# The order of two sweeps over keys and values across heads, and where their sums are divided

## The chip, the cores and the metric

The kernel runs on one core of a Trainium2 chip. The metric is the device time of one launch in microseconds (us). A core has TensorE (PE, matrix products, with PEld for its weight loads), VectorE (DVE), ScalarE (ACT), GpSimd (POOL) and SyncE (SP), which here only starts DMA transfers. Each engine runs its own list of instructions in order; they wait for one another by semaphores.

## What is computed

Two transformer blocks on 896 tokens (16 x 56) of width 256 with a context of 24000 rows (16 x 1500). The change concerns the first block's cross attention and the projection behind it. All queries see all keys, in 16 heads of width 16, with values, keys, queries and attention weights rounded to 8 bits:

```python
q = _fq_sym(q, axis=-1)
k = _fq_sym(k, axis=-1)
v = _fq_sym(v, axis=2)
attn = jnp.einsum('bhqd,bhkd->bhqk', q, k)
attn = jax.nn.softmax(attn.astype(jnp.float32), axis=-1)
attn = _fq_unsigned(attn, axis=-1)
out = jnp.einsum('bhqk,bhkd->bhqd', attn, v)
out = jnp.transpose(out, (0, 2, 1, 3)).reshape(B, N, C)
return out @ Wp + bp
```

`_fq_unsigned` scales each row of weights by its own largest one, so every query's maximum over all 24000 keys is needed before its weights can be rounded. After this come a mixture of experts with 34 experts, a scan over the context (done here beside the last head), and a second mixture.

## The kernel before

Stages follow one another with a barrier between: queries, keys and values, `attention` (650 to 4994 us of the profile), `first_block` (normalisation, projection, experts), `second_block`. The change touches `attention` and the start of `first_block`.

**Two sweeps.** Each head is swept twice over its keys. The first sweep finds each query's maximum; the second makes the weights and multiplies them with the values. They run side by side: while head h1 is in its first sweep, head h2 = h1 - 1 is in its second. A sweep has 8 chunks (NCH) of 24 steps (CT), 192 steps for a head; a step is one tile of 125 keys.

**Second sweep, per step.** PE makes two score products (448 queries each, L719) into three rotating banks; ACT takes their exponential into `e` (L911); POOL rounds both halves into `r` (L1114); five to six steps later (LAG) PE adds 12 products into the sums `psav` (L746 and L753), which hold four partial sums: two sets of steps and two halves of the queries, 17 rows each, the last of them the softmax's denominator. The exponential's shift comes in as six extra rows of `q2`.

**First sweep.** Per chunk 42 pieces (UNITS): one product of 128 queries with 500 keys (L731) into one of four rotating banks `ps1`, and its maximum by DVE (L968). `pieces` spreads them over the steps: in ordinary chunks over all 24 (7 in 4 steps), in chunk 0 over steps 2 to 23, and in chunk 7 over steps 0 to 17. Then DVE reduces the head's maxima and splits the shifts into three bf16 parts (`shifts`, L980 to L989), PE turns them into rows at step 22 (`shift_rows`, L783), and DVE copies these into `q2` (L995). Twice a chunk PE and DVE also pass a correction of the values through a `ps1` bank (`sum_values`, L807, and `value_sums`, L1004, steps 15 and 19); these two marks serve below to cut the trace into chunks.

**Head change.** PE finishes the old head's sums in step 4, ACT copies them to `av` (`copy_sums`, L927, behind the exponentials of step 4), PE waits for that copy (L820), clears `psav` (L765) and goes on. After step 5, `turn_sums` multiplies `av` with a folding matrix `fold` (L773): that adds the two sets of steps and turns the result so that tokens lie on partitions. DVE divides by the denominators (`head_result`, L1032 and L1034), and ACT's queue stores the head's 16 columns in DRAM (`store_head`).

**Loop.** Heads 0 and 1 are written out; a hardware loop of 7 passes with two heads each follows, then the last head's second sweep alone, beside which DVE weighs the context for the second block. SP's list loads, per chunk, the first sweep's keys, the values, the second sweep's keys, and in chunk 0 both query tiles.

**First block.** It loads the stored rows `h` (896 KB), multiplies them by the values' scales on DVE (L1374), turns them with 16 products (L186), copies them (L192) and projects.

## Time and profile before

| | us |
|---|---|
| median of three runs | 5639.08 |
| lowest, highest | 5627.64, 5639.2 |
| profiled execution | 5629.81 |
| its span, first to last instruction | 5628.5 |
| stage `attention` in it | about 4344 |

The page gives each engine's busy share, the clock granted to TensorE in slices, and costly groups of instructions. The stage table gives the same for any window. A timeline lists instructions in order of time; an idle time stands in brackets, with what ended it (`PEq L709` is PE's own list at a wait in line 709). All times below are from the one profiled execution.

### The profile page before, as it was taken

Reading aid. Unit: us, or ns where it says so; the run is one execution under the profiler, and the core shown is the slowest. Engines: PE = TensorE matmul, PEld = TensorE weight load, DVE = VectorE, ACT = ScalarE, POOL = GpSimd, SP = SyncE. Lnnn points to the kernel's source line nnn. Section 1 sums busy time; section 2 is a strip of 40 time slices with the busy share of each in tenths; the row PEclk is TensorE's granted clock in tenths of the full one; section 3 lists DMA queues with packets and bytes.
Section 4 is the critical chain, followed back from the end, with each engine's and each line's share of the span. In section 5 each row is a group of like instructions: output and inputs, shape, how many; then the busy total and the mean of one; then the engine's idle time right before and its main releaser. Section 6 shows DMA issues by size and latency. Waiting matters only on the chain. (4 is left out here: it accounts for less than half of the span.)

```text
span 5628.5 us, 168594 instructions
## 1 busy us (share of the span) xinstructions
PE 5190.6 (92%) x53204; PEld 1990.4 (35%) x53204; DVE 4323.5 (77%) x7292; ACT 3881.7 (69%) x6380; POOL 3599.3 (64%) x3762
## 2 busy tenths in 40 slices
PE   4888599999999999999999999999999999969969
PEld 2444222333333333333333333333333332225535
DVE  6888698988989898898989888898988862234444
ACT  1444305988989898898989899898989985620000
POOL 1555604877878787787878788788878876620000
PEclk8999657999999999999999999999999985559979
DMA  2655311111111111111111111111111112211101
GB/s 83 182 180 182 106 44 28 32 27 33 30 30 32 28 32 27 33 27 32 30 29 32 27 29 30 28 32 33 27 33 28 31 44 78 78 40 30 31 16 29
DMA packets 242806, 267.97 MB, mean 48 GB/s; under 512 B 48397, under 2 KB 223645, under 8 KB 241946
## 3 DMA queue, kind: packets, MB, share of 16 engines
q1 hardware_dynamic: 176570, 202.39, 14.4%
q10 hardware_dynamic: 65376, 54.68, 3.1%
q8 instruction: 471, 7.72, 0.6%
q14 instruction: 389, 3.19, 0.2%
HBM read 173.41 MB, written 82.06 MB: 45 GB/s over the span
## 5 line engine op out<-in xcount | busy, mean ns | idle before, releaser
L911 ACT ACTIVATE e<-ps_sweep,sk 125x448 f32<-125x448 f32 x6144 | 3543.8, 631 | 525.3 <-ACTq L910 432.4
L968 DVE TENSOR_REDUCE unit_max<-ps_sweep 128x1 f32<-128x500 f32 x5376 | 3243.2, 669 | 409.1 <-DVEq L967 363.2
L1114 POOL TENSOR_SCALAR r<-e 125x896 f32<-125x896 f32 x3072 | 2882.2, 952 | 852.7 <-POOLq L1113 484.2
L719 PE MATMUL ps_sweep<-q,k 54*128 54x448 bf16 x6144 | 2067.9, 371 | 34.7 <-PEq L709 24.8
L731 PE MATMUL ps_sweep<-k,q 48*128 48x500 bf16 x5376 | 1771.9, 394 | 48.8 <-PEq L730 36.5
L753 PE MATMUL ps_av<-e,zt 126*17 126x224 f32 x24576 | 1810.5, 372 | 0.0
L746 PE MATMUL ps_av<-r,vt 125*16 125x224 f16 x12288 | 875.2, 275 | 14.7 <-PEq L739 4.8
L731 PEld LDWEIGHTS ps_sweep<-k,q 48*128 48x128 bf16 x5376 | 362.3, 94 | 1269.6 <-issue 1256.8
L719 PEld LDWEIGHTS ps_sweep<-q,k 54*128 54x128 bf16 x6144 | 551.6, 94 | 703.9 <-issue 611.0
L753 PEld LDWEIGHTS ps_av<-e,zt 126*17 126x17 f32 x24576 | 648.1, 98 | 6.0 <-issue 1.1
L746 PEld LDWEIGHTS ps_av<-r,vt 125*16 125x16 f16 x12288 | 302.1, 86 | 837.0 <-issue 837.0
L397 PE MATMUL ps_kv<-wkv,cx 128*125 128x512 f32 x768 | 353.0, 614 | 18.6 <-PEq L395 18.6
L1268 ACT ACTIVATE gate<-ps_gate 96x896 f32<-96x896 f32 (+1 forms) x50 | 45.6, 913 | 414.7 <-ACTq L1267 414.7
L1004 DVE COPY zt<-ps_sweep 32x192 f32<-32x192 f32 x256 | 93.1, 364 | 287.4 <-DVEq L1003 285.5
L1436 POOL MEMSET sel<- 16x896 f32 x1 | 0.8, 835 | 416.1 <-POOLq L71 416.1
L1122 POOL TENSOR_TENSOR vr<-vr,v_inv 125x192 f32<-125x192 f32 x256 | 151.7, 593 | 173.0 <-issue 164.1
L467 POOL TENSOR_TENSOR kq<-kparts,k_scale 125x1024 f32<-125x1024 bf16 x48 | 96.7, 2014 | 203.7 <-POOLq L466 203.7
L1276 DVE TENSOR_TENSOR hid<-ps_up,gate 96x896 f32<-96x896 f32 (+1 forms) x50 | 54.3, 1087 | 223.6 <-DVEq L1275 223.6
L491 ACT ACTIVATE kparts<-kq 125x1024 bf16<-125x1024 f32 x48 | 50.7, 1057 | 246.7 <-ACTq L490 246.7
L1130 POOL TENSOR_SCALAR vt<-vr 125x192 f16<-125x192 f32 x256 | 219.6, 858 | 0.5 <-POOLq L1128 0.3
L397 PEld LDWEIGHTS ps_kv<-wkv,cx 128*125 128x125 f32 x768 | 146.8, 197 | 189.9 <-issue 189.9
L406 PE MATMUL ps_krows<-ident_b,kparts 125*128 125x125 bf16 x1536 | 107.6, 236 | 106.6 <-PEq L403 106.6
(184 smaller groups left out, 2645.4 us busy)
## 6 DMA issues: line engine op xcount, KB each, us to landing
k_rows<-krows ACTq DMA_DIRECT2D x48, 1000.0 KB, 6.6
k<-k_rows SPq DMA_DIRECT2D x128, 281.2 KB, 4.0
k<-k_rows SPq DMA_DIRECT2D x384, 93.8 KB
cx<-in_ctxT SPq DMA_DIRECT2D x48, 500.0 KB, 4.4
v_raw<-kv SPq DMA_DIRECT2D x24, 1000.0 KB
vr<-v_raw SPq DMA_DIRECT2D x128, 187.5 KB
cb<-in_ctxT SPq DMA_DIRECT2D x16, 1500.0 KB, 6.4
gu_w<-in_gu SPq DMA_DIRECT2D x34, 192.0 KB, 2.3
```

The source lines that it names most:

```text
L397: last = pe.matmul(psk[:, i, :], cx[u][:, c, i * KT:(i + 1) * KT], wkv[:, c, :], start=(c == 0), stop=(c == NC - 1))
L406: last = pe.transpose(pst[:, b, i, 0:KT], parts[u][:, i, b * P:(b + 1) * P], ident_b[0:KT, 0:KT])
L467: pool.tensor_tensor(q4, ints(u), per_head(of_step(k_scale, n)), ALU.mult).then_inc(kq_ready, 1)
L719: pe.matmul(ps2[(2 * i + g) % 3][:, 0:HALF], k2[u][:, i * KT:i * KT + P], q2[y][:, g * HALF:(g + 1) * HALF], start=True, stop=True, tile_p ...
L731: pe.matmul(ps[:, 0:SB], q1[y][rows, b * QB:(b + 1) * QB], k1[u][rows, at * SB:(at + 1) * SB], start=True, stop=True, tile_position=(ROWS1 ...
L746: last = pe.matmul(psav[c:c + HDIM, lo:hi], vt[u][:, i + s, :], words[:, g, 2 * lo:2 * hi:2], start=False, stop=False, skip_group_check=Tr ...
L753: last = pe.matmul(psav[c:c + WIDE, lo:hi], zt[u][0:ONES_ROW + 1, i + s, :], e[(i + s) % SLOTS][0:ONES_ROW + 1, g, lo:hi], start=False, st ...
L911: act.activation(e[i % SLOTS][0:KT, g, :], ps2[(2 * i + g) % 3][0:KT, 0:HALF], ACT.Exp, scale=sk[u][:, i:i + 1]).then_inc(e_wrote, 1)
L968: top = dve.tensor_reduce(unit_max[:, b, bass.ds(j * NPIECE + at, 1)], ps[:, 0:SB], axis=AX.X, op=ALU.max)
L1114: pool.tensor_scalar(r[i % SLOTS][:, :, :], e[i % SLOTS][0:KT, :, :], 1.0, HALFWORD, ALU.mult, ALU.add)\
L1122: pool_done(pool.tensor_tensor(part, part, v_inv[:, bass.ds(h * HDIM, HDIM)].rearrange("p (o d) -> p o d", o=1) .to_broadcast([KT, VTILES, ...
L1130: pool_done(pool.tensor_scalar(vt[u][:, tiles, :], vr[:, tiles, :], ROUND, ROUND, ALU.add, ALU.subtract))
```

## The change

**Order of the first sweep.** The 336 pieces of a head are no longer dealt out by chunk. The last 12 steps of a head, 180 to 191, are taken out: in nine of them (EARLY) one piece of the *following* head is made, so that 327 pieces of a head remain for its steps 0 to 179 (MAIN). Right after the head's last piece, at step 180, DVE starts the shifts, now in three portions at steps 180, 181 and 183 with early pieces between, and PE turns them at the end of step 186. The values' corrections move to steps that have one piece. In the first head, 336 pieces are dealt over its steps 0 to 179.

**Sums.** `fold`, `turn_sums`, `head_result` and `store_head` go. ACT copies `psav` one step earlier in its list (before the exponentials of step 4), and SP stores the copy unturned: eight DMAs a head, issued in chunk 2, of four 16 x 448 sums and four rows of denominators. `first_block` loads them (1.8 MB), adds the two sets, inverts the denominators, spreads them over each head's 16 rows by a product with a selection matrix, multiplies, and has the values' scales in the projection's weights `wp` instead.

**Loop.** Six passes instead of seven; heads 14 and 15 are written out behind it, since head 15 has no follower (`more` false).

**SP's list.** Both query tiles of a head were loaded in chunk 0 behind the second sweep's keys; now the first sweep's come right behind its keys, and the second sweep's (which wait until the head before has left the tile) in chunk 1.

```diff
+    SCORES = NCH * UNITS
+    EARLY = (1, 0, 1, 0, 1, 1, 0, 1, 1, 1, 1, 1)
+    STEPS = NCH * CT
+    MAIN = STEPS - len(EARLY)
+    TURNED = len(EARLY) // 2
...
-        def pieces(i, at, end):
-
-            return 0 if i < at else min(UNITS, -(-UNITS * (i + 1 - at) // (end - at)))
-
-        def span_of(second, head_start, last):
-            return START if head_start and second else 0, CT - (LAG + 1 if last else 0)
+        def pieces(step, second, more):
+            ahead = sum(EARLY) if second else 0
+
+            def done(n):
+                return ahead - (-(SCORES - ahead) * n // MAIN)
+            if step < MAIN:
+                return [(False, n) for n in range(done(step), done(step + 1))]
+            lo = sum(EARLY[:step - MAIN])
+            return [(True, n) for n in range(lo, lo + EARLY[step - MAIN])] if more else []
+
+        def value_steps(j, second, more):
+            few = [i for i in range(SLOTS + 7, CT) if len(pieces(j * CT + i, second, more)) < 2]
+            return (few[0], few[-1]) if len(few) > 1 else (SLOTS + 7, CT - 2)
...
+            def store_sums(h):
+                sp.wait_ge(av_kept, 1).then_inc(av_kept, -1)
+                for c in range(4):
+                    sp.dma_start(attn_sums[c // 2, c % 2, bass.ds(h * HDIM, HDIM), :],
+                                 av[c * QUAD:c * QUAD + HDIM, :]).then_inc(av_stored, 16)
+                    sp.dma_start(attn_z[c, bass.ds(h, 1), :], av[c * QUAD + HDIM:c * QUAD + WIDE, :])\
+                      .then_inc(av_stored, 16)
...
             over_heads(sp, head)
+            store_sums(HEADS - 1)
+            sp.wait_ge(av_stored, 128).then_inc(av_stored, -128)
...
             def copy_sums():
                 act.wait_ge(sums_done, 1).then_inc(sums_done, -1)
+                act.wait_ge(av_stored, 128).then_inc(av_stored, -128)
                 act.activation(av[:, :], psav[:, 0:HALF], ACT.Copy).then_inc(av_ready, 1)
...
-                            if i == LAG - 1:
-                                copy_sums()
-                            if i == LAG + 3:
-                                store_head(finished)
+                        if head_start and finished is not None and i == LAG - 2:
+                            copy_sums()
...
+                        if first and step == MAIN:
+                            head_max(h1)
+                        if first and step == MAIN + 1:
+                            high_part()
+                        if first and step == MAIN + 3:
+                            other_parts()
...
+            pe.wait_ge(z_ready, 1).then_inc(z_ready, -1)
+            for c in range(NC):
+                for g in range(2):
+                    last = pe.matmul(ps[:, 2 * c + g, 0:HALF], head_sel[:, c * P:(c + 1) * P], z[0][:, g, :],
+                                     start=True, stop=True)
...
             dve.wait_ge(bp_landed, 16).then_inc(bp_landed, -16)
-            dve.wait_ge(attn_landed, 16).then_inc(attn_landed, -16)
-            dve.tensor_tensor(h[:, :, :], h[:, :, :], over_tokens(v_scale[0:TT, :], DIM), ALU.mult)\
-               .then_inc(a_ready, 1)
-            dve.wait_ge(a_turned, 1).then_inc(a_turned, -1)
-            copy_transposed(hT, ps).then_inc(aT_ready, 1)
+            dve.wait_ge(z_landed, 32).then_inc(z_landed, -32)
+            dve_done(dve.tensor_tensor(z[0][:, :, :], z[0][:, :, :], z[1][:, :, :], ALU.add))
+            dve.reciprocal(z[0][:, :, :], z[0][:, :, :]).then_inc(z_ready, 1)
+            dve.wait_ge(w_landed, 32).then_inc(w_landed, -32)
+            dve.wait_ge(scales_turned, 1).then_inc(scales_turned, -1)
+            for c in range(NC):
+                last = dve.tensor_tensor(wp[:, c, :], wp[:, c, :], psb[:, 0, c:c + 1].to_broadcast([P, DIM]), ALU.mult)
+            dve_done(last)
+            dve.wait_ge(attn_landed, 64).then_inc(attn_landed, -64)
+            dve_done(dve.tensor_tensor(attn[0][:, :, :, :], attn[0][:, :, :, :], attn[1][:, :, :, :], ALU.add))
+            dve.wait_ge(z_spread, 1).then_inc(z_spread, -1)
+            for c in range(NC):
+                last = dve.tensor_tensor(hT[:, c, :].rearrange("p (g n) -> p g n", g=2), attn[0][:, c, :, :],
+                                         ps[:, 2 * c:2 * c + 2, 0:HALF], ALU.mult)
+            last.then_inc(aT_ready, 1)
```

DVE's list at the end of a head's first sweep in the loop's first head. Before, with the maxima of this head (L968), the shifts (L980 to L989), a values' correction (L1004) and the copies into `q2` (L995):

```order
L968 TENSOR_REDUCE unit_max<-ps_sweep_3 128x1
L980 TENSOR_REDUCE run_max<-unit_max 128x7
L981 ISA
L981 TENSOR_TENSOR shift<-run_max,sq 128x7
L983 TENSOR_SCALAR shift<-shift 128x7
L984 CAST shift_parts<-shift 128x7
L985 TENSOR_TENSOR shift<-shift,shift_parts 128x7
L986 CAST shift_parts<-shift 128x7
L987 TENSOR_TENSOR shift_parts<-shift,shift_parts 128x7
```

Now, where the maxima (L973) between are already the following head's:

```order
L973 TENSOR_REDUCE unit_max<-ps_sweep_0 128x1
L985 TENSOR_REDUCE run_max<-unit_max 128x7
L986 ISA
L986 TENSOR_TENSOR shift<-run_max,sq 128x7
L988 TENSOR_SCALAR shift<-shift 128x7
L973 TENSOR_REDUCE unit_max<-ps_sweep_1 128x1
L991 CAST shift_parts<-shift 128x7
L992 TENSOR_TENSOR shift<-shift,shift_parts 128x7
L973 TENSOR_REDUCE unit_max<-ps_sweep_2 128x1
L995 CAST shift_parts<-shift 128x7
L996 TENSOR_TENSOR shift_parts<-shift,shift_parts 128x7
```

The shifts begin six steps earlier and are cut apart by two maxima; four maxima of the next head stand ahead of the copies into `q2`.

PE's list around the turning of the shifts at the end of the loop's second head. Before, with scores (L719), sums (L746, L753) and the shifts' products (L783):

```order
L746 MATMUL ps_av<-r,vt 16x224 x4
L753 MATMUL ps_av<-e,zt 17x224 x4
L719 MATMUL ps_sweep_0<-q_0,k_1 128x448
L783 MATMUL ps_sweep_1<-ident_b,shift_parts 6x128 x4
L783 MATMUL ps_sweep_2<-ident_b,shift_parts 6x128 x3
L719 MATMUL ps_sweep_1<-q_0,k_1 128x448
L746 MATMUL ps_av<-r,vt 16x224 x4
L753 MATMUL ps_av<-e,zt 17x224 x4
L719 MATMUL ps_sweep_2<-q_0,k_1 128x448
L624 REGISTER_ALU
L624 COMPARE_AND_BRANCH
```

Now, with scores (L747), sums (L777, L784), the shifts' products (L810) and pieces of the next head (L762):

```order
L762 MATMUL ps_sweep_3<-k_0,q_0 128x500
L747 MATMUL ps_sweep_2<-q_0,k_1 128x448
L747 MATMUL ps_sweep_0<-q_0,k_1 128x448
L777 MATMUL ps_av<-r,vt 16x224 x4
L784 MATMUL ps_av<-e,zt 17x224 x4
L747 MATMUL ps_sweep_1<-q_0,k_1 128x448
L810 MATMUL ps_sweep_0<-ident_b,shift_parts 6x128 x4
L810 MATMUL ps_sweep_1<-ident_b,shift_parts 6x128 x3
L747 MATMUL ps_sweep_2<-q_0,k_1 128x448
L777 MATMUL ps_av<-r,vt 16x224 x4
L784 MATMUL ps_av<-e,zt 17x224 x4
L762 MATMUL ps_sweep_2<-k_0,q_0 128x500
```

The products stand five steps ahead of the head's end instead of one, and pieces stand before and behind them.

PE's list in steps 5 and 6 of the loop's second head. Before, with the clearing (L765) and the folding (L773):

```order
L765 MATMUL ps_av<-zeros 32x448 x4
L746 MATMUL ps_av<-r,vt 16x224 x4
L753 MATMUL ps_av<-e,zt 17x224 x4
L731 MATMUL ps_sweep_2<-k_0,q_1 128x500
L719 MATMUL ps_sweep_2<-q_0,k_0 128x448
L773 MATMUL ps_sweep_3<-fold,av 112x64 x2
L773 MATMUL ps_sweep_0<-fold,av 112x64 x2
L731 MATMUL ps_sweep_1<-k_0,q_1 128x500
```

Now:

```order
L801 MATMUL ps_av<-zeros 32x448 x4
L777 MATMUL ps_av<-r,vt 16x224 x4
L784 MATMUL ps_av<-e,zt 17x224 x4
L762 MATMUL ps_sweep_0<-k_0,q_1 128x500
L747 MATMUL ps_sweep_2<-q_0,k_0 128x448
L762 MATMUL ps_sweep_1<-k_0,q_1 128x500
L747 MATMUL ps_sweep_0<-q_0,k_0 128x448
```

The folding is gone from between the pieces; the wait for the copy ahead of the clearing stays.

## Rows read from the trace of the kernel before

**Rows 1.** Page: clock granted to TensorE, 40 slices of the span, tenths.

```profile
PEclk8999657999999999999999999999999985559979
```

**Rows 2.** Stages: window, its us, busy us (instructions) per engine, clock, DMA share, GB/s.

```profile
2404.06:2577.43 173.37, 172.76 (x2281) 62.70 (x2280) 157.30 (x265) 164.76 (x288) 149.35 (x169) 1.00 0.14 31
...
2577.43:2610.08 32.65, 32.22 (x392) 11.08 (x389) 30.95 (x53) 28.84 (x50) 26.26 (x30) 1.00 0.14 31
...
3859.15:3894.00 34.85, 31.42 (x390) 11.93 (x390) 25.79 (x51) 27.95 (x50) 24.22 (x28) 1.00 0.15 30
...
2366.74:2404.06 37.32, 33.94 (x390) 12.78 (x390) 26.21 (x52) 27.88 (x50) 24.14 (x28) 0.91 0.13 28
...
2610.08:2654.94 44.86, 38.10 (x390) 12.86 (x390) 26.44 (x52) 28.08 (x50) 24.45 (x28) 0.77 0.12 25
```

**Rows 3.** Line L980 on DVE, one a head: ns min/median/max, first and last start.

```profile
L980 DVE TENSOR_REDUCE run_max<-unit_max x16: 502/502/504, 897.7 to 4594.2; 128x7 f32<-128x336 f32 x16
```

**Rows 4.** PE timeline, the undisturbed head change: start, us, line, tiles, [idle before].

```profile
3868.70 0.55 PE L783 MATMUL ps_sweep<-ident_b,shift_parts 128*6 128x128 bf16 x7 [1.00 <-PEq L781]
...
3871.22 0.35 PE L719 MATMUL ps_sweep<-q,k 54*128 54x448 bf16 x1 [0.80 <-ACT e L911]
...
3877.58 0.37 PE L731 MATMUL ps_sweep<-k,q 48*128 48x500 bf16 x1 [0.64 <-DVE unit_max L968]
...
3879.41 0.37 PE L765 MATMUL ps_av<-zeros 125*32 125x448 bf16 x4 [0.72 <-PEq L820]
...
3880.62 1.00 PE L773 MATMUL ps_sweep<-fold,av 128*112 128x64 f32 x8
```

**Rows 5.** DVE timelines: end of the first head (POOL idle), and of two later heads.

```profile
898.98 0.18 DVE L984 CAST shift_parts<-shift 128x7 bf16<-128x7 f32 x1
...
2371.16 0.50 DVE L980 TENSOR_REDUCE run_max<-unit_max 128x7 f32<-128x336 f32 x1 [0.42 <-DVEq L91]
...
2373.12 0.96 DVE L984 CAST shift_parts<-shift 128x7 bf16<-128x7 f32 x1
...
2375.81 0.17 DVE L989 COPY shift_parts<-shift_parts 128x7 bf16<-128x7 bf16 x1
...
2588.89 21.16 DVE L968 TENSOR_REDUCE unit_max<-ps_sweep 128x1 f32<-128x500 f32 x36 [0.44 <-PE ps_sweep L731]
```

**Rows 6.** Stages: four steps of a denser chunk 0, and of an ordinary one.

```profile
2404.06:2409.26 5.20, 5.20 (x67) 1.86 (x65) 5.14 (x10) 4.80 (x9) 4.66 (x6) 1.00 0.01 3
...
2433.03:2438.04 5.01, 4.91 (x66) 1.85 (x64) 4.57 (x9) 4.63 (x9) 4.47 (x6) 1.00 0.00 0
```

**Rows 7.** PE timeline, first score after the loop's branch.

```profile
2625.45 0.53 PE L719 MATMUL ps_sweep<-q,k 54*128 54x448 bf16 x1 [3.76 <-PEq L709]
```

**Rows 8.** Stages: one chunk of the last head, second sweep alone.

```profile
4733.30:4779.22 45.92, 45.92 (x339) 10.50 (x338) 10.13 (x12) 27.94 (x48) 29.49 (x29) 0.50 0.24 80
```

**Rows 9.** PE timeline, first turn of the key scales in the first head.

```profile
700.81 1.04 PE L797 MATMUL ps_sweep<-ident_b,t_parts 125*128 125x125 bf16 x8 [20.80 <-PEq L791]
```

**Rows 10.** SP timeline: three issues in a row.

```profile
2628.16 1.24 SPq L650 DMA_DIRECT2D k<-k_rows  x3
```

**Rows 11.** Timeline from the last sums to the next stage, all engines.

```profile
4985.03 0.55 ACT L927 ACTIVATE av<-ps_av 128x448 f32<-128x448 f32 x1 [5.99 <-ACTq L926]
...
4988.89 1.86 PE L892 MATMUL ps_sweep<-ctx_sum,w_in 128*128 128x16 f32 x8 [2.06 <-PEq L889]
...
5003.28 2.29 DVE L1374 TENSOR_TENSOR h<-h,v_scale 112x2048 f32<-112x2048 f32 x1 [9.43 <-DVEq L1373]
...
5009.09 2.09 DVE L192 COPY hT<-ps_a 128x896 f32<-128x896 f32 x2 [3.51 <-DVEq L1376]
```

**Rows 12.** DMA issues around there: tiles, queue, count, KB each, us to landing.

```profile
h<-attn_rows SPq DMA_DIRECT2D x1, 896.0 KB, 7.5
...
w_out<-in_W_outT SPq DMA_DIRECT2D x1, 256.0 KB, 3.9
```

**Rows 13.** A reciprocal of 256 columns on DVE.

```profile
L1016 DVE RECIPROCAL v_inv<-v_scale x1: 1753/1753/1753, 872.2 to 872.2; 125x256 f32<-125x256 f32 x1
```

198 lines of the change are left out of this document (89 added, 109 removed).

## The prediction

> **What bounds the kernel now.** Read the page's clock row first: TensorE has nearly full clock through the loop, and half in the first and the last head [rows 1]. Then the stage table, then the timelines at a head change. In an ordinary stretch everything is full: six chunks between the same mark (L1004) of chunk 0 and chunk 6 take 173.37 us, 28.90 us a chunk or 1.204 us a step, and PE is busy for 172.76 us of them at full clock (first row of [rows 2]). ACT stands close behind: 164.76 us for 288 exponentials, 0.572 us each, so 1.144 us for the two of a step; DVE has 157.30 us. Nothing in the change shortens such a step.
>
> Sixteen heads' reductions start 3696.5 us apart from first to last [rows 3], 246.4 us a head. Eight ordinary chunks would be 231.2 us. The other 15.2 us a head are the subject. They lie in two places [rows 2]. From chunk 6's mark to chunk 7's it takes 32.65 us, 3.75 too long: 42 maxima are asked for in 18 steps, and DVE runs 36 of them without a gap in 21.16 us, 0.588 us each [rows 5], more than PE needs. From chunk 7's mark to the next head's it takes 34.85, 37.32 or 44.86 us: 5.95, 8.4 or 16.0 too long, 11.5 us as a mean over the heads (15.2 - 3.75).
>
> The undisturbed change (34.85 us, clock 1.00) opens up in [rows 4]: PE waits 1.00 us for the shifts, turns them for 0.55, waits 0.80 for ACT, whose supply had run dry, 0.64 at the end of the sums, 0.72 for the copy, clears `psav` for 0.31 (3879.41 to the next sums) and folds for 1.00: 5.0 of the 5.95. In the 37.32 row the same idle times are followed by a granted clock of 0.91, 1.2 GHz for a part of the stretch; that is the other 2.5 us. In the 44.86 row PE also stands 3.76 us behind the loop's branch [rows 7] and the mean clock is 0.77. What a half clock costs: a chunk of the last head, all at 0.50, takes 45.92 us [rows 8], 1.913 us a step against 1.204, so 0.37 us lost in each us spent there.
>
> **The change, part by part.** The sum is made against the profiled 5629.8 us, 9.3 below the median of the runs.
>
> *Maxima of chunk 7.* The squeeze goes: -3.75 a head.
>
> *Shifts.* On DVE they take from 2371.16 to 2375.98 [rows 5], 4.8 us. Now they start at step 180 and PE asks for them at the end of step 186, seven steps or 8.1 us later at 1.15 each. Ahead of their end stand two early maxima (1.2 us): 0.7 us of lag, 4.8 and 1.2 are 6.7 us. So PE does not wait, ACT does not run dry, and only the 0.55 us of products stay: -1.8 a head, and -0.6 more for what follows them. What is late next is DVE's copy into `q2`, but five steps with early pieces stand between it and the head's start.
> The cast L984 takes 0.96 us there and 0.18 us where POOL has nothing to do [rows 5]. The Trainium skill (SBUF — State Buffer, "SBUF: two separate sides") says that VectorE and GpSimd share one port pair as an exclusive lock held for the whole instruction, which would explain that; by it the shifts would still wait for POOL's roundings in their new place, and the trace's 4.8 us already has such waits in it.
>
> *Early pieces and density.* Nine pieces in twelve steps leave PE free to follow ACT: 12 x (1.204 - 1.15) = -0.6. The price is that 327 pieces stand in 180 steps, where the old spacing would have 315: twelve more. Two stretches of four steps price one more maximum: with ten DVE instructions 5.20 us, with nine 5.01 [rows 6], so 0.19 us, and 12 x 0.19 = +2.3 a head. Bounds: a maximum costs nothing where ACT sets the pace (a little under 0.1 by the spread between steps with one and two pieces), and 0.588 us where DVE has no gap. DVE would be busy for 26.2 + 1.6 x 0.588 = 27.2 us of a 29 us chunk, so it is nearer to the first.
>
> *Sums.* Folding goes (-1.00), and the copy one place earlier in ACT's list ends before PE asks for it (-0.7). The end of the sums (0.64) and the clearing (0.31) stay, with a little around them: I keep 1.6 us a head. Less idle time also means, I expect, no half clock at a change without a branch: the stretch that stayed at 1.00 had the same waits as those that fell, and of these only one is left. SP's eight issues a head cost 8 x 0.42 us [rows 10] in chunk 2, where its next load has most of a chunk to spare: nothing. The moved query loads: `q1` is issued around step 157 and needed at 180; nothing.
>
> *A head after it:* 231.2 + 2.3 - 0.6 + 0.55 + 1.6 = 235.05 us. With a branch in front: 3.8 us of stall and some 11 us at half clock (4.1): 243.0. There are five branches taken instead of six. The first of the 15 heads has no sums to end but starts at half clock, as the 0.7 of the slice from 844 to 985 us has it [rows 1], for about 13 us (+4.8): 238.2. Together 238.2 + 9 x 235.05 + 5 x 243.0 = 3568.7 against 3696.5: **-127.8**.
>
> *Start of the stage.* DVE no longer builds `fold`, and pieces can start some 8 us earlier, but PE then waits for the scales' parts from POOL, 20.80 us before [rows 9]: it only waits longer. Four early maxima delay the first head's shifts, two pieces more are made before that wait: +1.
>
> *Last head.* No shifts' wait before it and no folding, so some of its first steps run at full clock instead of half, about 7 x 0.7, and the wait and folding go; the values' corrections come up to four steps later, which delays DVE's weighing and SP's next loads by up to 4 us once. **-6**, between -20 (full clock until those loads are late) and +4.
>
> *End of the stage.* SP used to issue the last biases and weights before the sums were done; PE could use them at 4988.89 [rows 11]. Now SP first waits for the copy (ends 4985.58), issues eight stores (8 x 0.45 = 3.6), sees them land (2.5, less than the 3.9 us of a 256 KB load [rows 12]), issues four loads (1.8) and waits for the last (3.9): 4997.4. **+8**.
>
> *Start of the first block.* Before, multiply, turn and copy take from 5003.28 to 5011.18, 7.9 us [rows 11]. Now DVE's list first waits for `bp`, which is the last issue of nine, behind 1 MB more than before; at the 896 KB in 7.5 us of [rows 12], with 0.3 MB ahead of it, that is about +6. Then it adds the denominators (1.0), inverts 896 columns (256 take 1.75 [rows 13], so 6.1), scales `wp` (0.8), adds 1792 columns (2.0, from 2.29 us for 2048) and multiplies 2 x 896 (2.1), with gaps 13.0, so +5. Less for longer rows per packet: **+10**.
>
> Sum: -127.8 + 1 - 6 + 8 + 10 = **-115**. 5629.8 - 115 = 5515 for the profiled execution, and 5639.1 - 115 = **5524 us** against the median.
>
> **The rivals.**
> (a) *The half clock stays at plain head changes.* For it: 0.64 us of idle and the clearing remain, and 37.32 was reached in most changes. Against: the other waits go. 10 x 2.5 = +25: 5549.
> (b) *The denser maxima are DVE's bound.* Every one of the twelve costs 0.588 instead of 0.19, since DVE's gaps are latencies between it and PE and do not shrink: 12 x 0.4 x 15 = +72: 5596. For it: the squeezed chunk. Against: [rows 6].
> (c) *The shifts are late again.* POOL's lock or a DVE that lags by three pieces makes PE wait 1 to 2.5 us a head: about 5550.
> (d) *The clock falls in the early stretch: slower than before.* With nine pieces in twelve steps PE is used less than in ordinary steps, and the last head, with none, never leaves 0.50 [rows 8]. If the clock fell at step 180 of each head, the 12 steps would cost 12 x 0.75 = 9 us and the recovery some 7 us x 0.37 = 2.6: 11.6 x 15 = +174, less 13 already counted at the branches: 5685. It decides as soon as the fall comes in more than two heads of three. Against: before, six steps with no piece at all stand at full clock in the 34.85 us row, in spite of 1.8 us of idle.
> The Trainium skill (TensorE: Matmul & The Clock Gate, "A second HAM failure mode: psum-queue depth-cycling") says that frequent small idle times of PE between groups of matmuls can make its clock alternate between the two levels; by that rule (d) is what the early stretch would do.
> (e) *It does not do what it says:* a queue (SP behind `av_kept`, or `q1`) blocks an early piece, and the gain is eaten: about 5630.
>
> **How the numbers follow.** Forecast 0.57, (a) 0.16, (b) 0.12, (c) 0.06, (d) 0.05, (e) 0.04. The forecast's own spread: density at 0.1 us saves 16 more, the last head up to 14, the branches 10 either way, which gives 5480 below; above, (a), (c) and nearly all of (b) are inside 5592. Range 5480 to 5592. About 0.2% (11 us) is what a measurement of this kernel can tell from no change. Faster by more than that: the forecast, (a), (b), (c) and a part of (e), 0.92; within it 0.02; slower 0.06.
>
> **What would show it.** In the changed profile: reductions of a head's maxima about 235 us apart without a branch and 243 with one; ordinary chunks of 29.0 to 29.4 us; no idle time before the shifts' products; PE's clock row without dips at plain changes; idle before the clearing under 0.3 us; the last weights' product about 8 us later behind the copy, and the projection's start 10 later behind the barrier. Wrong would be: chunks of 29.8 us with DVE gapless (b), clock under 0.9 in steps 180 to 191 (d), PE waiting at the shifts (c).

## The result, and the profile of the changed kernel

The changed kernel takes 5470.15 us (median of 4, 5466.69 to 5472.06) against 5639.14 us for the kernel before (5627.64 to 5651.59): ratio 0.9699, 95% interval 0.9678 to 0.972. It is 169 us faster. The forecast had 115, and its range ended at 5480. The profiled execution of the changed kernel spans 5465.5 us, 163.0 less than the span of before, 5628.5; the other 6 us come from how far the two profiled executions lie from their medians.

The page's clock row looks like that of [rows 1]: 9 in every slice inside the loop, in both kernels, because a dip of 7 to 24 us is lost in a slice of 137 to 141 us. The first and the last head still stand at half clock. So the dips have to be read from the windows below:

```profile
PEclk8999756999999999999999999999999985569979
```

The line that corresponds to [rows 3] (one reduction of a head's maxima, on DVE):

```profile
L985 DVE TENSOR_REDUCE run_max<-unit_max x16: 502/503/505, 892.9 to 4424.5; 128x7 f32<-128x336 f32 x16
```

From first to last it is 3531.6 us instead of 3696.5, 235.4 us a head instead of 246.4. For the account of where the time went I use a mark that stands at the same step of a head in both kernels, PE's clearing of the sums (its first matmul in each head; columns of the line: ns min/median/max, first and last start). The first of the two lines is the kernel before, where the line number is L765, the second the changed kernel:

```profile
L765 PE MATMUL ps_av<-zeros x64: 349/532/556, 910.2 to 4614.0; 125*32 125x448 bf16 x64
```

```profile
L801 PE MATMUL ps_av<-zeros x64: 349/363/556, 909.6 to 4445.0; 125*32 125x448 bf16 x64
```

Start of the stage -0.6; fifteen heads 3703.8 to 3535.4, **-168.4**; from the last clearing to ACT's copy of the last sums (4985.03 in [rows 11], 4805.83 now) 371.0 to 360.8, **-10.2**; from there to the first product of the projection (5011.33 before, 4848.05 now) 26.3 to 42.2, **+15.9**; from there to the end +0.2. These make -163.1, the difference of the spans up to rounding.

The stage rows that correspond to [rows 2]: the six chunks 1 to 6 of a head, a whole head without a branch in front, and one with it (columns as in [rows 2]). The fourth is the 23 us around a branch, the fifth the 22 us around a plain head change:

```profile
3767.99:3942.12 174.13, 173.03 (x2292) 62.28 (x2291) 161.22 (x274) 164.37 (x289) 149.67 (x169) 1.00 0.13 32
3255.76:3489.62 233.86, 231.31 (x3053) 83.25 (x3053) 211.75 (x364) 219.65 (x385) 199.53 (x225) 1.00 0.13 32
3489.62:3729.63 240.01, 234.16 (x3052) 83.30 (x3052) 212.37 (x364) 220.24 (x385) 199.78 (x225) 0.99 0.13 31
...
1596.87:1620.00 23.13, 18.70 (x222) 6.28 (x225) 13.58 (x23) 15.58 (x28) 13.68 (x16) 0.85 0.12 32
3729.63:3752.00 22.37, 21.44 (x277) 7.76 (x276) 17.21 (x29) 19.90 (x35) 17.64 (x21) 1.00 0.12 31
```

The plain change stands at clock 1.00. Around the branch 0.85 over 23.13 us is 6.9 us at 1.2 GHz; the row of a branch before, 44.86 us at 0.77 [rows 2], had 20.6 us of it. Over all fifteen heads, from the first clearing to the last, the clock records of the traces have 208.5 us at 1.2 GHz before and 34.2 us now. At the 0.37 us lost in each us (from [rows 8], in a head without pieces), an estimate, that is some 64 of the 168.4 us. The rows of these two windows, the kernel before first:

```profile
910.25:4614.03 3703.78, 3619.20 (x45871) 1291.43 (x45871) 3214.46 (x5524) 3326.02 (x5777) 2998.49 (x3361) 0.97 0.14 31
```

```profile
909.55:4444.98 3535.43, 3485.05 (x45747) 1249.72 (x45747) 3170.04 (x5427) 3297.69 (x5775) 2993.51 (x3361) 1.00 0.13 32
```

The waits of [rows 4] have shrunk to one of 0.81 us (PE timeline of a plain change, and the branch's stall below it):

```profile
3743.95 0.37 PE L762 MATMUL ps_sweep<-k,q 48*128 48x500 bf16 x1 [0.81 <-PEq L761]
```

```profile
1607.88 0.57 PE L762 MATMUL ps_sweep<-k,q 48*128 48x500 bf16 x1 [3.62 <-PEq L761]
```

Except in the first head (1.72 us) there is no wait before the shifts' products (L810 below has no brackets), since DVE has the parts ready at 1128.17, 1.65 us earlier (DVE's timeline of the same head end). The cast L991 takes 0.44 us here, against 0.96 in [rows 5]:

```profile
1129.82 0.55 PE L810 MATMUL ps_sweep<-ident_b,shift_parts 128*6 128x128 bf16 x7
```

```profile
1122.90 0.50 DVE L985 TENSOR_REDUCE run_max<-unit_max 128x7 f32<-128x336 f32 x1 [0.42 <-DVEq L91]
...
1124.89 0.44 DVE L991 CAST shift_parts<-shift 128x7 bf16<-128x7 f32 x1
...
1128.00 0.17 DVE L998 COPY shift_parts<-shift_parts 128x7 bf16<-128x7 bf16 x1
```

### The profile page after: what moved, and what is told of

Same layout as the page of the kernel before. It is cut to its first block and busy times, and to the rows that moved or that the text cites. A ratio compares the mean times of both kernels' runs of the same rounds, so it can differ in the third digit from the quotient of the medians.

```text
span 5465.5 us, 168195 instructions
## 1 busy us (share of the span) xinstructions
PE 5042.0 (92%) x53072; PEld 1945.4 (36%) x53072; DVE 4278.0 (78%) x7199; ACT 3852.2 (70%) x6380; POOL 3597.7 (66%) x3766
## 5 line engine op out<-in xcount | busy, mean ns | idle before, releaser
L973 DVE TENSOR_REDUCE unit_max<-ps_sweep 128x1 f32<-128x500 f32 x5376 | 3235.0, 669 | 364.2 <-DVEq L972 344.9
L747 PE MATMUL ps_sweep<-q,k 54*128 54x448 bf16 x6144 | 2033.3, 366 | 9.6 <-PEq L737 4.1
L762 PE MATMUL ps_sweep<-k,q 48*128 48x500 bf16 x5376 | 1749.8, 391 | 59.8 <-PEq L761 54.2
L784 PE MATMUL ps_av<-e,zt 126*17 126x224 f32 x24576 | 1771.8, 365 | 0.0
L777 PE MATMUL ps_av<-r,vt 125*16 125x224 f16 x12288 | 866.2, 272 | 28.6 <-PEq L770 18.8
L762 PEld LDWEIGHTS ps_sweep<-k,q 48*128 48x128 bf16 x5376 | 349.5, 94 | 1253.2 <-issue 1248.5
L747 PEld LDWEIGHTS ps_sweep<-q,k 54*128 54x128 bf16 x6144 | 556.5, 94 | 650.3 <-issue 538.0
L784 PEld LDWEIGHTS ps_av<-e,zt 126*17 126x17 f32 x24576 | 639.8, 97 | 4.3 <-issue 0.9
L777 PEld LDWEIGHTS ps_av<-r,vt 125*16 125x16 f16 x12288 | 302.1, 85 | 811.0 <-issue 810.9
L407 PE MATMUL ps_krows<-ident_b,kparts 125*128 125x125 bf16 x1536 | 106.9, 235 | 106.7 <-PEq L404 106.7
```

The source lines that it names most:

```text
L407: last = pe.transpose(pst[:, b, i, 0:KT], parts[u][:, i, b * P:(b + 1) * P], ident_b[0:KT, 0:KT])
L747: pe.matmul(ps2[(2 * i + g) % 3][:, 0:HALF], k2[u][:, i * KT:i * KT + P], q2[y][:, g * HALF:(g + 1) * HALF], start=True, stop=True, tile_p ...
L762: pe.matmul(ps[:, 0:SB], q1[y][rows, b * QB:(b + 1) * QB], k1[u][rows, at * SB:(at + 1) * SB], start=True, stop=True, tile_position=(ROWS1 ...
L777: last = pe.matmul(psav[c:c + HDIM, lo:hi], vt[u][:, i + s, :], words[:, g, 2 * lo:2 * hi:2], start=False, stop=False, skip_group_check=Tr ...
L784: last = pe.matmul(psav[c:c + WIDE, lo:hi], zt[u][0:ONES_ROW + 1, i + s, :], e[(i + s) % SLOTS][0:ONES_ROW + 1, g, lo:hi], start=False, st ...
L973: top = dve.tensor_reduce(unit_max[:, b, j * NPIECE + at:j * NPIECE + at + 1], ps[:, 0:SB], axis=AX.X, op=ALU.max)
```

## The experiments

Theory: the clock no longer falls at plain changes (those without a branch in front), as forecast, and the heads gained more than forecast because it stays down for a shorter time behind a branch and because the denser list of maxima costs nearly nothing. Rivals: the gain is that of the sums alone; the corrections' new steps hide the density; the last head is what saved the most. The medians were not all measured together: that of the kernel before, run again beside each group, moved between 5630 and 5639 us, and the four or five times of one kernel lie 2 to 17 us apart. So for each small difference the traces' marks are given beside it.

| kernel | us | ratio to before (95%) | against 5470.2 |
|---|---|---|---|
| old order of maxima | 5576.9 | 0.9904 (0.9881 to 0.9927) | +106.7 |
| none ahead | 5502.9 | 0.9769 (0.9747 to 0.9791) | +32.7 |
| fixed corrections | 5480.4 | 0.9729 (0.9710 to 0.9748) | +10.3 |
| slow copy | 5535.6 | 0.9823 (0.9799 to 0.9846) | +65.5 |
| three passes | 5453.5 | 0.9682 (0.9668 to 0.9697) | -16.6 |
| values first | 5455.4 | 0.9686 (0.9671 to 0.9700) | -14.8 |
| spare products | 5643.7 | 1.0021 (1.0006 to 1.0036) | +173.5 |
| loads, then stores | 5459.1 | 0.9693 (0.9677 to 0.9708) | -11.0 |
| wide spares (one run) | 5370.4 | | -99.7 |
| no weighing (one run) | 5330.1 | | -140.1 |
| empty first steps | 5489.0 | 0.9752 (0.9734 to 0.9770) | +18.9 |
| three changes | 5432.6 | 0.9651 (0.9634 to 0.9669) | -37.6 |
| all, with spares | 5346.6 | 0.9479 (0.9442 to 0.9516) | -123.6 |
| copy's place | 5516.2 | 0.9774 (0.9734 to 0.9814) | +46.0 |
| five ahead | 5495.0 | 0.9743 (0.9704 to 0.9782) | +24.9 |

**The order of the maxima alone undone.**

```
-                        if first and step == MAIN:
-                            head_max(h1)
...
+                        if first and last and i == end - 1:
+                            head_max(h1)
+                            high_part()
+                            other_parts()
```

(and `pieces` and `span_of` of the kernel before, with the corrections at steps 15 and 19)

> The changed kernel (5470 us) with the order of maxima and shifts of before: 42 maxima a chunk, chunk 7 squeezed into 18 steps, shifts asked for at step 190; sums stay unturned, loop of six passes. By the terms of the prediction the order of maxima was worth 3.75 (squeeze) + 2.4 (shifts) + 0.6 (early steps) a head, less the density. With the density at 0.7 us a head, as the chunks of the changed kernel have it (29.0 instead of 28.9 us), that is 6.0 a head: 5560 us if the clock stays up at plain head changes, and some 2.5 more a plain change, 5585, if it falls there again as it did before. Rival: the sums made nearly all of the gain (the idle at the head change went with the folding), and this kernel stands under 5520. I expect 5570.

Measured 5576.9, near the 5570 expected. Its first and last clearing (same line as above, for this kernel) are 3648.3 us apart:

```profile
L790 PE MATMUL ps_av<-zeros x64: 349/363/556, 908.2 to 4556.5; 125*32 125x448 bf16 x64
```

So of the 168.4 us in the heads 112.9 are the order of the maxima (7.5 a head), and 55.5 (3.7 a head) the unturned sums together with the one branch less. Neither half made the gain by itself. Six chunks of this kernel, with 252 maxima, take as long as six with 262 in the changed kernel, 174.07 us against 174.13:

```profile
3863.63:4037.70 174.07, 173.26 (x2281) 62.16 (x2281) 156.87 (x265) 164.81 (x289) 149.46 (x169) 1.00 0.14 31
```

The difference between the two orders thus lies in chunk 7 and the chunk after it: by the starts of the scores in PE's timelines chunk 7 takes 36.0 us here and 30.8 in the changed kernel, chunk 0 33.6 and 31.0 (means of 13 heads). And the clock still falls here at six of the ten plain changes: in the window of 25 us around one of them it is 0.86, 7.0 us at half clock. Over all fifteen heads this kernel has 123.2 us at half clock, between the 208.5 of before and the 34.2 of the changed kernel, so both parts of the change take a share of it away.

```profile
2355.00:2380.00 25.00, 22.87 (x256) 7.36 (x252) 15.16 (x29) 18.61 (x33) 15.29 (x17) 0.86 0.17 39
```

The waits in it, from PE's timeline, are the one before the shifts and the one for ACT:

```profile
2363.44 0.55 PE L799 MATMUL ps_sweep<-ident_b,shift_parts 128*6 128x128 bf16 x7 [0.67 <-PEq L797]
2365.97 0.53 PE L736 MATMUL ps_sweep<-q,k 54*128 54x448 bf16 x1 [0.80 <-ACT e L921]
```

**No piece ahead, five ahead.** `EARLY = (0,) * 12`, and `EARLY = (1, 0, 0, 0, 1, 0, 0, 1, 0, 1, 0, 1)`.

> The changed kernel with no piece ahead: all 336 maxima of a head stand in its first 180 steps, and steps 180 to 191 have none, with the shifts in the same place. This is the test for the price of a maximum and for the clock in a stretch with few pieces. Theory 1 (a maximum more in an ordinary chunk costs about 0.06 us, because ACT and PE set the pace, and the clock does not mind 12 steps without pieces): 15 heads x 9 maxima x 0.06 = +8, so 5478 us, with PE's granted clock at 1.00 over plain head changes. Rival (b) of the prediction (0.59 us each): +80, 5550. Rival (d) of the prediction (the clock falls in steps 180 to 191): +9 to +12 a head, 5610 or more, with a granted clock under 0.9 there.

> The changed kernel with five pieces ahead instead of nine, so 331 instead of 327 in the first 180 steps (44.1 a chunk). From 42 to 43.6 a chunk the ordinary chunk grew by 0.1 us, from 43.6 to 44.8 by 0.3 to 0.7. If the price of a maximum grows bit by bit: 4 x 0.1 x 15 = +6, 5476 us. If there is a point past which each costs DVE's 0.59 us, and it lies just above 43.6: 4 x 0.5 x 15 = +30, 5500 us. If it lies nearer to 44.8: 5472 us.

**Corrections at fixed steps.**

```
-            return (few[0], few[-1]) if len(few) > 1 else (SLOTS + 7, CT - 2)
+            return SLOTS + 7, SLOTS + 11
```

> The changed kernel with the values' corrections back at steps 15 and 19 of a chunk, where they stand beside two maxima, instead of at steps with one. If the density was cheap only because the change moved the corrections to thin steps, the ordinary chunks grow from 29.0 to 29.3 us or more (0.19 us x 12 = 2.3 a head less the 0.7 seen): 15 x 1.6 = +24, 5494 us. If the density is cheap by itself: 5470 less about 5, because in the last head the second correction comes up to four steps earlier, and with it DVE's weighing and SP's next loads: 5465 us.

**No maxima in a head's first two steps.**

```
-                return ahead - (-(SCORES - ahead) * n // MAIN)
+                lag = 2 if second else 0
+                return ahead - (-(SCORES - ahead) * max(0, n - lag) // (MAIN - lag))
```

> The changed kernel with no maxima asked for in the first two steps of a head, as before the change (327 pieces in 178 steps instead of 180). In the changed kernel the half clock behind a branch lasts 3.4 to 6.8 us, before it lasted 14 to 24, and with the old order of maxima and the new sums 10 to 20. If it is the pieces in the first steps behind the branch that bring the clock back early: half clock of 10 us and more behind each of the five branches, +2 to 4 us each, and perhaps falls at some plain changes: 5470 + 10 to 40, I expect 5490 us. If it is the shifts' wait ahead of the branch, now gone, that made it long: the half clock stays at 3.4 to 6.8 us, and only the density costs something (0.5 a head): 5475 us.

These four belong together. Chunks 1 to 6 of the same head, one row each: fixed corrections, empty first steps, five ahead, none ahead. Against them stand 174.13 us of the changed kernel above, and 173.37 in [rows 2].

```profile
3780.22:3954.97 174.75, 173.68 (x2291) 62.31 (x2290) 161.65 (x275) 164.73 (x289) 149.56 (x169) 1.00 0.13 32
```

```profile
3783.21:3958.42 175.21, 173.91 (x2294) 62.80 (x2292) 163.28 (x278) 165.24 (x289) 149.34 (x169) 1.00 0.13 32
```

```profile
3788.34:3964.18 175.84, 174.86 (x2294) 62.28 (x2294) 163.66 (x278) 164.95 (x289) 149.72 (x169) 1.00 0.13 32
```

```profile
3795.88:3972.25 176.37, 175.20 (x2300) 62.99 (x2299) 165.33 (x282) 164.77 (x289) 149.40 (x169) 1.00 0.14 34
```

Counted by PE's pieces (L762) between the first scores of chunk 1 and chunk 7, these six chunks have 262 maxima in the changed kernel and with fixed corrections, 264 with empty first steps, 265 with five ahead and 269 with none. The DVE column has the 12 corrections beside them, and one or two instructions at the edges. Up to 262 they cost nothing that could be measured; two more cost 1.1 us and three 1.7, 0.5 to 0.6 each; seven cost 2.2, 0.3 each.

With the corrections back at steps 15 and 19 the six chunks grow by 0.6 (0.8 as the median over 13 heads). The kernel with the old order has its corrections there too, and 252 maxima in 174.07 us; so with the corrections in their old place ten maxima cost 0.7 us, 0.07 each, and the corrections' new places save just that. The run came out between its two cases (5494 by the rival, 5465 by mine, 5480 measured): the density is cheap by itself, and with the moved corrections it is free. Five ahead costs nearly as much as none ahead (24.9 and 32.7 us), and 5495.0 is near the 5500 us that had been set for a price that jumps just above the changed kernel's density; so above 262 the price is more a step than a slope. None ahead came 25 us above the 5478 expected. It is not DVE being full either: DVE is busy for 165.33 of 176.37 us.

What makes the step is open. One explanation fits only in part: a chunk with fewer than two steps of a single maximum behind step 14 has its corrections at steps 15 and 22, beside two maxima. With five ahead that is so in chunks 0 to 3, which grow by 0.1 to 0.4 us each, while 5 and 6 grow by 0.0 and 0.2. But chunk 4 grows by 0.5 all the same; chunks 1 and 6 of the changed kernel itself have their corrections at 15 and 22 beside two maxima and take 29.0 us like the others; and with empty first steps chunk 2 grows by 0.75 us with both corrections at steps of one maximum. So moving the corrections is shown to save 0.6 us in six chunks; that the single maximum beside them is the reason is not shown.

None ahead also disposes of rival (d): twelve steps without any piece leave PE's clock at full speed at every plain change. The empty first steps came out at 5489.0 us, with 5490 expected, but for the most part by the other term: a plain head takes 234.7 instead of 233.8 us, 14 of the 19 us, by density; the heads behind a branch grow by 1.6, so the missing pieces behind a branch cost 0.7 us each and not 2 to 4. What made the half clock 20.6 us long before was therefore for the most part not the lack of pieces there.

**The copy later and longer, and the copy in the place of before.** The first copies three times, with waits between, at `i == LAG - 1`; the second only changes the place (this line stands in both):

```
-                        if head_start and finished is not None and i == LAG - 2:
+                        if head_start and finished is not None and i == LAG - 1:
```

> The changed kernel with ACT copying the sums one place later in its list and three times over, so that PE waits some 2.3 us longer before it clears them, once in each of the 15 heads that has sums to end and not at the end of the stage alone. If an idle time costs only itself: +35, 5505 us, PE's clock at 1.00 over plain changes. If idle time of this size at the change brings the clock down, as it stood in most changes of before (2.5 us and more each): +70 to +100, 5540 to 5570 us, with dips in the clock after every copy. I expect the dips.

> The changed kernel with ACT's copy of the sums one place later in its list, where the kernel before has it. PE then has two waits at a change, 0.6 to 0.8 us at the end of the sums and some 0.7 more before it clears them. With 2.5 us before the clearing the clock fell at every change; with 0.64 and nothing before the clearing at none. If two waits of 0.7 are too little to bring the clock down: 14 x 0.7 = +10, 5480 us, no dips at plain changes. If the place of the copy was what made the dips of before: +10 and 9 plain changes x 2.5 more, 5503 us or above, with dips in the clock row of the records.

Measured +65.5 and +46.0: both bring the dips back at every one of the 15 changes with sums to end. In the first the wait before the clearing is 2.5 us and a head takes 4.1 us longer (3597.2 from first to last clearing), 1.6 more than the wait. The window over a plain change of the second has clock 0.86 in 24.00 us, 6.7 us at half clock, and these waits of PE (the fall begins in the second of them). Of the other eight plain changes between two heads, one has the same 6.8 us at half clock, and seven have 3.4 us:

```profile
4000.00:4024.00 24.00, 21.89 (x257) 7.04 (x250) 17.36 (x30) 18.32 (x33) 15.36 (x18) 0.86 0.08 21
```

```profile
4007.76 0.37 PE L762 MATMUL ps_sweep<-k,q 48*128 48x500 bf16 x1 [0.64 <-PEq L761]
4009.92 0.57 PE L801 MATMUL ps_av<-zeros 125*32 125x448 bf16 x4 [1.19 <-PEq L796]
```

Of the two cases set down, 5480 us without dips and 5503 or above with them, the second came. The wait is 1.2 us instead of 0.7, and the clock falls between 0.9 us ahead of its end and 1.7 us behind it. The heads take 36.8 us longer (2.45 a head): 1.2 of each head is the wait itself, the rest what comes with the fall. Another 11 us are the last head's, which then begins at half clock (the profiled executions are 49 us apart, the medians 46). So one place in ACT's list, which the forecast booked at -0.7 a head, is worth 46 us.

**Three passes of four heads.**

```
-            with eng.Fori(0, (HEADS - 4) // 2) as hd:
-                for y in range(2):
-                    head(hd * 2 + 2 + y, hd * 2 + 1 + y, hd * 2 + y, y, True)
+            with eng.Fori(0, (HEADS - 4) // 4) as hd:
+                for y in range(4):
+                    head(hd * 4 + 2 + y, hd * 4 + 1 + y, hd * 4 + y, y % 2, True)
```

> The changed kernel with four heads in the loop's body and three passes instead of two and six: two branches taken back instead of five, everything else in the same order. A head with the branch in front of it measured 239.4 us and one without 233.8, so a branch is worth 5.6 us (stall and the short half clock behind it): -17, 5453 us. Rival: a body twice as long brings stalls of its own, in which an engine waits for instructions, and nothing is won: 5470 us.

Measured -16.6 us, and the clearings stand 3519.3 us apart instead of 3535.4, 16.1 less: 5.4 us a branch. The longer body brings no new stall.

**The last head.** SP's loads of the values and keys of a chunk go ahead of the context's loads:

```
-                        load_context(j * 2, 0)
-                        load_context(j * 2 + 1, 1)
+                        for b in {0: (0, 1), 1: (), NCH - 1: range(2 * NCH - 4, 2 * NCH)}.get(j, (2 * j - 2, 2 * j - 1)):
+                            load_context(b, b % 2)
```

> The changed kernel, in the last head of which SP issues the context loads behind the values' and keys' loads of the next chunk, instead of ahead of them. The values of a chunk then no longer wait for DVE's weighing: the wait of 12.1 us at 4498 goes, and some 2.5 us of smaller ones. Theory A (the last head fell to half clock because of those waits): the clock stays up through the last head, its chunks take 29 instead of 46 us, and the time is 5470 - 13 - 100 = 5360 us. Theory B (it falls because that head has no pieces, and the waits only come at the same time): -13 alone, 5457 us. I expect B.

In the changed kernel the last head begins at full clock and keeps it for 32 us; then PE waits 1.53 us and a little later 12.13 (PE timeline; the windows below are the stretch before the fall and one behind it):

```profile
4475.31 0.28 PE L777 MATMUL ps_av<-r,vt 125*16 125x224 f16 x4 [1.53 <-PEq L772]
...
4498.38 0.36 PE L777 MATMUL ps_av<-r,vt 125*16 125x224 f16 x4 [12.13 <-PEq L770]
```

```profile
4444.98:4476.80 31.82, 29.54 (x364) 10.41 (x368) 10.48 (x7) 28.57 (x52) 28.88 (x29) 1.00 0.01 2
...
4600.00:4640.00 40.00, 40.00 (x299) 9.02 (x297) 9.76 (x11) 24.27 (x43) 25.67 (x25) 0.50 0.28 91
```

With the values first the wait of 12.13 us goes and the last head takes 349.5 instead of 360.8 us. The wait of 1.5 stays, and behind it PE is busy for 298.34 of 300 us at clock 0.50 without ever coming back. The reason of that wait is in this kernel's POOL timeline, seven roundings in 13.39 us beside DVE's weights (L1030 to L1038), 1.91 us each, against 0.94 just before. The second of them takes 3.89 us and ends 0.73 us behind DVE's scan (L1031); the next begins beside DVE's reduction of one input (L1032, from 4473.23 to 4474.95) and takes 0.93:

```profile
4468.55 13.39 POOL L1104 TENSOR_SCALAR r<-e 125x896 f32<-125x896 f32 x7 [0.17 <-POOLq L1101]
```

```profile
4469.93 3.89 POOL L1104 TENSOR_SCALAR r<-e 125x896 f32<-125x896 f32 x1
...
4473.79 0.93 POOL L1104 TENSOR_SCALAR r<-e 125x896 f32<-125x896 f32 x1
```

```profile
4469.32 3.77 DVE L1031 TENSOR_TENSOR_SCAN weight<-keep,ones_c 128x1500 f32<-128x1500 f32 x1
```

The Trainium skill (SBUF — State Buffer, "SBUF: two separate sides") says that a VectorE instruction of certain kinds and a GpSimd one hold the port pair that they share for their whole length, and the other blocks. The rows agree with that: the rounding that started beside the scan ended only behind it, and the one beside the reduction was not held up.

**Spare products** in the last head, 64 rows wide, three in two steps; and wide ones, two a step:

```
+                pe.matmul(ps1[0][0:2 * QUAD, 0:SB], q1[1][ROWS1:ROWS1 + HROWS, 0:2 * QUAD],
+                          k1[1][ROWS1:ROWS1 + HROWS, 0:SB], start=True, stop=True, tile_position=(ROWS1, 0))
```

```
+                    pe.matmul(ps1[0][:, 0:SB], q1[1][ROWS1:ROWS1 + HROWS, 0:QB],
+                              k1[1][ROWS1:ROWS1 + HROWS, 0:SB], start=True, stop=True, tile_position=(ROWS1, 0))
```

> As with the values' loads ahead of the context's, and in the last head PE also makes three products every two steps that nobody reads (64 rows by 500 columns, from the last head's queries and keys), in the place of the pieces that this head has not. Theory B (the last head stands at half clock because PE is used less there than with pieces): the clock is held up, a step costs 1.15 to 1.2 us as in an ordinary chunk, 8 chunks take 230 instead of 360 us, and the time is 5470 - 125 = 5345 us. If the spare products do not hold the clock: 288 products at about 0.42 us (half clock, 500 columns) come on top of a head that PE bounds, +120: 5580 us.

> The kernel with the values' loads first (5455 us), and in the last head two spare products a step that nobody reads, from its fourth step on, each as wide as a real piece (128 rows by 500 columns; the earlier spares had 64 rows, one and a half a step, began with a wait for all four banks of 1.08 us, and there the clock fell at once and never came back). If what the last head lacks is pieces, and the earlier test missed that because its spares were narrower and fewer or because of its wait: the clock stays up and the last head takes some 235 us instead of 360: 5335 us. If spares, however wide, do not hold the clock once DVE's weighing has held up POOL's roundings and PE has waited for them: the clock falls some 40 us into the head as before, and 384 products at 0.4 us and more come on top: 5640 us.

**No weighing.** The values' loads first, and without DVE's weights and weighing (this kernel leaves out a part of the computation, so its time only serves the argument):

> The kernel with the values' loads first, which leaves out the weights and the weighing of the context on DVE (the context's sum is zero and the loads are only taken in). In the last head seven of POOL's roundings took 13.39 us beside DVE's weights, 1.91 us each instead of 0.94, PE waited 1.54 us for them, and the clock fell at the end of that wait. If that wait is the cause, the clock stays up through the last head: 192 steps at 1.15 to 1.2 us are 225 us instead of 357, and the time is 5455 - 130 = 5325 us. If the clock falls because that head has no pieces: it falls in its first 60 us all the same, and the time stays at 5455 less 5 (the last two weighings lie beside the end of the head).

The narrow spares came out at 5643.7 us, above even the 5580 set down for spares that do not help: PE's wait for all banks, 1.08 us at the head's start, brought the clock down at once, and then 440 us with PE busy all the time stay at 0.50 (first row). The wide spares hold it: 0.95 over the last head, 263.1 us instead of 349.5, with a few short falls behind waits for POOL, each followed by full clock (second row). Without the weighing there are no spares, no pieces, and no fall: 226.0 us at 1.00 (third row).

```profile
4460.00:4900.00 440.00, 440.00 (x2464) 104.46 (x2464) 67.66 (x78) 200.45 (x317) 180.47 (x187) 0.50 0.14 50
```

```profile
4444.50:4707.60 263.10, 233.01 (x3069) 80.70 (x3069) 91.34 (x99) 214.25 (x377) 240.87 (x217) 0.95 0.28 96
```

```profile
4442.00:4668.00 226.00, 219.38 (x2695) 78.19 (x2695) 5.25 (x16) 210.59 (x376) 193.50 (x217) 1.00 0.31 112
```

POOL's seven roundings near the same place take 6.35 us in that kernel, 0.91 each:

```profile
4457.00 6.35 POOL L1096 TENSOR_SCALAR r<-e 125x896 f32<-125x896 f32 x7 [0.54 <-POOLq L1093]
```

So both theories of these runs were half right. The fall comes with the waits that DVE's work brings about, not from the lack of pieces (I had expected the opposite): without that work, and with no pieces either, there is none. After a fall the clock came back with the wide spares and did not with the narrow ones or with none. The two kinds of spares differ in width, in number and in the wait at the start, so which of these decides is open. The kernels with wide spares and without the weighing were each run once; the wide spares' gain came again in the last kernel of the table, which has four runs.

**The end of the stage.** The last biases and weights ahead of the last stores:

```
+            store_sums(HEADS - 1)
+            sp.wait_ge(av_stored, 128).then_inc(av_stored, -128)
```

(behind the issue of `w_out` instead of ahead of the waits for free buffers)

> The changed kernel with the last biases and weights issued ahead of the last head's eight stores, as in the kernel before, instead of behind them. The prediction gave +8 us for the stage's end behind the stores, and the traces have +5.4 there. If that is right: 5465 us, with the product with the last weights (L906) about 3 to 5 us behind the copy of the sums instead of some 10. Rival: the stores, now behind 0.75 MB of loads, land as late as the weights did, the barrier waits for them, and nothing changes: 5470 us.

In the changed kernel the product with the last weights, L906, waits for loads that SP issues behind the stores; the rows are from the timeline of the stage's end, first the changed kernel, then this one:

```profile
4805.83 0.54 ACT L942 ACTIVATE av<-ps_av 128x448 f32<-128x448 f32 x1 [5.30 <-ACTq L941]
...
4812.51 0.47 SPq L729 DMA_DIRECT2D w_out<-in_W_outT  x1
...
4815.81 1.86 PE L906 MATMUL ps_sweep<-ctx_sum,w_in 128*128 128x16 f32 x8 [10.63 <-PEq L903]
```

```profile
4807.16 0.54 ACT L942 ACTIVATE av<-ps_av 128x448 f32<-128x448 f32 x1 [5.52 <-ACTq L941]
...
4808.65 1.37 PE L906 MATMUL ps_sweep<-ctx_sum,w_in 128*128 128x16 f32 x8 [2.13 <-PEq L903]
...
4839.27 9.13 PE L199 MATMUL ps_b<-wp,hT 128*112 128x256 f32 x32 [2.38 <-PEq L1376]
```

From the copy to the projection it is 32.1 us instead of 42.2, 10.1 less. That is more than the 5 I expected: L906 alone comes 8.5 us sooner behind the copy (1.5 us instead of 10.0), and the way from it to the projection is 1.6 us shorter.

**Together.**

> Three passes of four heads, the values' loads first in the last head, and the last loads ahead of the last stores, together. Alone they took 17, 15 and 11 us off the 5470 us. They lie in three different places, so they should add up: 5427 us, faster than both kernels. Rival: the last head's 15 us and the end's 11 us overlap, because the last loads then wait for the queue behind the last context loads: 5437 us.

> The last head with wide spare products and the values' loads first (one look: 5370 us), with three passes of four heads and the last loads ahead of the last stores. These two took 17 and 11 us off the changed kernel alone, and together with the values' loads 38 of the 43 that their sum is. If they add up here as well: 5370 - 17 - 10 = 5343 us, 5% under the kernel before. Rival: with the last head's end no longer at half clock the last loads are late behind the context's, and the end gives nothing: 5353 us.

5432.6 and 5346.6 us. The first lies midway between the 5427 expected and the rival's 5437, the second at 3.6 us above the 5343 expected. Of the 42 us of the three changes 38 are there, so whether the last head and the end of the stage overlap a little is open; with the wide spares the kernel is 5.2% faster than before (ratio 0.9479, 0.9442 to 0.9516) and 124 us faster than the changed kernel.

## Why the prediction was wrong, point by point

The direction was right and so were most places. The sum was 48 us short against the profiled execution (5515 forecast, 5466.7 with what lies around the span), and 40.6 of it are in the heads. Two terms of the sum failed. The density of the maxima was put at 0.19 us each, +2.3 us a head; a maximum cost at most 0.07, and all that the ordinary chunks grew by is 1.0 us a head. The difference of 1.3 makes 18.6 us over 14 heads. The half clock behind a branch, put at 11 us, was 3.4 to 6.9: 11.1 us over five heads. The basis (7.3) and the first head (3.6) make up the rest of the 40.6.

- **Basis of the heads** (7 us). The 246.4 us a head were taken from reduction to reduction [rows 3]. That leaves out the beginning of the last head and takes in that of the first. From clearing to clearing the same fifteen heads of before take 3703.8 us, 7.3 more.
- **Heads behind a branch: 243.0 forecast, 239.5 measured** (five of them, 17.7 us). 1.3 of the 3.5 us a head are the density, as in the next point. The other 2.2 are the branch's own, 7.9 forecast and 5.7 measured. The stall was right (3.8 against 3.6 to 4.1). The mis-sized term is the half clock behind it: 11 us forecast, 6.9 in the window around the first branch, and in the clock records 6.8 at four branches and 3.4 at one. I had read 11 off the changes of before (10 to 24 us in their clock records), where the wait before the shifts, ACT run dry and the clearing's wait came within the same 20 us.
- **Plain heads: 235.05 forecast, 233.7 measured** (nine, 11.9 us). No half clock, as forecast, and rival (a) did not come. The failed term is the density, +2.3 a head. Eight chunks at the rate of the six measured (174.13) are 232.2 us, 1.0 more than 231.2. Of that the order of before with the new sums shows nearly all (174.07), so it is not the maxima that cost it; what does, 0.7 us in six chunks between the kernel before and that one, is open. My 0.19 us for a maximum compared two stretches of four steps [rows 6], a difference of 0.19 us that I took for the price of the maximum alone; measured over six chunks it is 0.07 with the corrections in their old place and, against the old order's chunks, about 0.01 in the new. The move of the corrections, worth 0.6 us in six chunks, was priced at nothing there. It also is not quite what was set down: in chunks 1 and 6 they still stand beside two maxima, at steps 15 and 22. The bound "nothing where ACT sets the pace" was the right end.
- **First head: 238.2 forecast, 234.6 measured.** Most of its half clock lies ahead of the first clearing.
- **Squeeze, shifts, early steps: right in kind, too small in sum.** 4.45 us a head by the forecast's terms (3.75, 2.4 and 0.6 less 2.3), 7.5 with the order undone. Without the density's 2.3 it is 6.75. The rest, 0.8 a head, I put down to the clock, which falls at six plain changes again when the shifts are waited for and stays down longer behind branches (89 us more at half clock in the fifteen heads); no run separates the two. Shifts' wait: gone, no rival (c). No gapless DVE, no rival (b), and up to 262 maxima in six chunks nothing of it.
- **Sums: -1.7 a head forecast,** measured only together with one branch less: 3.7 a head. The branch accounts for 0.3 to 0.7 of it, an estimate: 5.4 us now, and before between 4.9 (heads with and without a branch, from clearing to clearing) and 10.0 (44.86 against 34.85 us in [rows 2]), over 15 heads. What remains is more than the 1.7; the old order with the new sums has 85 us less at half clock than the kernel before. The term that I missed is that the copy's place decides on the clock: in its old place the heads take 2.45 us more each.
- **Start: +1 forecast, -0.6 measured**; nothing follows from it.
- **Last head: -6 forecast, -10.2 measured, by two large terms of opposite sign.** Full clock came at the start as forecast, and lasted for some 27 steps instead of 7 (32 us at 1.2 a step; at 0.7 us saved in each, -19). But PE then stood for 12.1 us waiting for values, where it stood for 4.8 before. The moved corrections, forecast as a delay of up to 4 us, are 2.9 of these 7.4 us more (9.3 with the corrections fixed). With the old order, too, it stands for 9.0, and with the copy in the place of before, where the last head begins at half clock, for 7.8: part of what the full clock won was given back, because PE came sooner to this wait and the loads did not. That "the last head, with none, never leaves 0.50" [rows 8] is owed to the lack of pieces alone was the wrong reading: without the weighing it stays at 1.00.
- **End of the stage +8 and start of the first block +10: +15.9 measured.** The last weights' product comes 10.0 us behind the copy's start (3.9 before), 6.1 of the 8; the rest is 9.8 of the 10. The reciprocal of 896 columns took 5.74 us, 6.1 estimated. The order of stores and loads gives back 10.1 of the 15.9.
- **Rival (d)** had 0.05 and did not come. The Trainium skill (TensorE: Matmul & The Clock Gate, "A second HAM failure mode: psum-queue depth-cycling") has small idle times between groups of matmuls make the clock alternate. The granted clock of the plain change, 1.00 with an idle time of 0.81 us, does not show that. The one with two waits, 0.64 and 1.19 us, does. So the trace agrees for the second alone.
- **The range** had -16 for the density, -14 for the last head and 10 either way for the branches. The 18.6 us of the density, the 11.1 of the branches, the first head, the basis and the 6 us between profiled executions and medians came together, all with the same sign.
